# Turning the attention values with VectorE and through DRAM, one item later

## The reference, cut to what matters

```python
x = x + _L1_conv_ref(_gn(x), ...)   # q, k, v of 1024 tokens, masked softmax(q k) v, then Wo
x = x + _L2_conv_ref(_gn(x), ...)   # qkv, softmax(q k + rel_h + rel_w) v per image, then proj
...
s = jnp.einsum('bhqe,bhke->bhqk', q, k) * scale
p = jax.nn.softmax(s, axis=-1)
return jnp.einsum('bhqk,bhke->bhqe', p, v)
```

## Time and profile before

| | |
|---|---|
| median of 3 runs | 1244.69 us |
| the profiled execution's own time | 1246.36 us |
| its span, first to last instruction | 1244.4 us |
| TensorE busy (matmul) | 1216.4 us, 98% |
| weight load, VectorE, ScalarE, GpSimd busy | 78%, 55%, 38%, 52% |
| mean granted TensorE clock | 0.997 of full speed |
| chain that ended last | TensorE 89%, VectorE 5%, ScalarE 2% |
| DMA | 155.03 MB, 125 GB/s mean |

### The profile page before, as it was taken

How to read it: one execution, slowest core, us unless ns; L and a number is a source line. 1 busy time by engine, 2 the same in 40 slices (tenths; PEclk the granted TensorE clock), 3 DMA queues, 4 the chain that set the end, 5 groups by cost and what they waited for, 6 DMA issues and landing times.

```text
span 1244.4 us, 19555 instructions
## 1 busy us (share of the span) xinstructions
PE 1216.4 (98%) x6768; PEld 975.0 (78%) x6768; DVE 690.4 (55%) x1434; ACT 475.1 (38%) x1229; POOL 641.5 (52%) x726
## 2 busy tenths in 40 slices
PE   6999999999999999999999999999999999889998
PEld 4788896478888888888888878777887787668887
DVE  7534444775665433666452578756347776476212
ACT  3611141034645320656341164644206555243212
POOL 4633389256565567555546655555665556464000
PEclk9999999999999999999999999999999999999999
DMA  5211124025564643454645356557535565620012
GB/s 185 84 46 48 34 56 117 8 65 160 154 169 137 184 134 97 127 177 128 185 136 166 86 160 212 180 160 223 168 102 151 175 209 156 205 60 1 29 40 68
DMA packets 129376, 155.03 MB, mean 125 GB/s; under 512 B 30080, under 2 KB 84000, under 8 KB 129280
## 3 DMA queue, kind: packets, MB, share of 16 engines
q1 hardware_dynamic: 118976, 146.92, 39.7%
q10 hardware_dynamic: 10304, 6.88, 1.8%
HBM read 111.81 MB, written 37.75 MB: 120 GB/s over the span
## 4 chain that ended last, share of the span: by engine, by line
PE 89%; DVE 5%; ACT 2%; issue 1%; DMA 1%; SPq 1%; POOL 0%; ACTq 0%; DVEq 0%; POOLq 0%
PE PS L1137 53%; PE PS L682 7%; PE PS L1758 7%; PE PS L1183 4%; PE PS L960 3%; PE PS L969 2%; PE PS L975 2%; PE PS L1227 2%; PE PS L1216 2%; PE PS L1775 2%; PE PS L1247 2%; PE PS L665 1%; PE PS L1197 1%; DVE bst L257 1%; PE PS L700 1%
## 5 line engine op out<-in xcount | busy, mean ns | idle before, releaser
L1137 PE MATMUL PS<-XB,w_hi 128*128 128x512 f32 x1024 | 340.5, 397 | 1.2 <-POOL w_lo L228 1.2
L226 POOL CAST w_hi<-w_raw 128x512 fp32r<-128x512 f32 x195 | 124.2, 637 | 307.5 <-PE PS L1137 213.0
L228 POOL TENSOR_TENSOR w_lo<-w_raw,w_hi 128x512 fp32r<-128x512 f32 x195 | 256.1, 1313 | 15.6
L1137 PEld LDWEIGHTS PS<-XB,w_hi 128*128 128x128 f32 x1024 | 192.2, 188 | 47.1 <-issue 5.0
L1137 PE MATMUL PS<-XB,w_lo 128*128 128x512 f32 x512 | 200.2, 391 | 0.0
L1137 PE MATMUL PS<-XB,part 128*128 128x512 f32 x768 | 190.3, 394 | 0.0
L1137 PEld LDWEIGHTS PS<-XB,part 128*128 128x128 f32 x768 | 141.9, 188 | 32.2 <-issue 2.3
L1373 ACT ACTIVATE part<-PS,nmax 128x256 f32<-128x256 f32 (+1 forms) x256 | 112.2, 443 | 141.6 <-DVE nmax L1485 93.2
L1383 ACT ACTIVATE part<-part,prec 128x256 f32<-128x256 f32 (+1 forms) x256 | 105.8, 476 | 27.7 <-DVE prec L1500 27.7
L228 POOL TENSOR_TENSOR part<-part,part 128x512 fp32r<-128x512 f32 x85 | 111.5, 1312 | 6.8
L1137 PE MATMUL PS<-part,w_hi 128*128 128x512 f32 x344 | 112.9, 395 | 1.5 <-DVE part L1544 1.5
(11 more groups left out here) (136 smaller groups left out, 1884.0 us busy)
## 6 DMA issues: line engine op xcount, KB each, us to landing
w_raw<-in_w SPq DMA_DIRECT2D x187, 256.0 KB, 2.8
part<-in_w SPq DMA_DIRECT2D x85, 256.0 KB, 2.8
turned<-part SPq DMA_DIRECT2D x128, 128.0 KB, 2.9
part<-turned SPq DMA_DIRECT2D x32, 512.0 KB, 5.0
turned<-part SPq DMA_DIRECT2D x128, 96.0 KB, 2.5
part<-turned SPq DMA_DIRECT2D x32, 384.0 KB, 4.0
strips<-part ACTq DMA_DIRECT2D x16, 256.0 KB, 2.7
out_x<-xT SPq DMA_DIRECT2D x16, 256.0 KB, 2.1
```

The lines of the kernel that those rows point to most:

```text
L226: pool.tensor_copy(hi, raw).then_inc(w_hi_done, 1)
L228: pool.tensor_tensor(lo, raw, hi.bitcast(F32), ALU.subtract).then_inc(w_ready, 1)
L1137: m = nc.tensor.matmul(PS[:, bank, :], wt[:, (c % 4) * P:(c % 4) * P + P], rhs(hl, c), start=c == k == 0, stop=c == CK - 1 and k == 2)
```

## The change

The values are no longer turned by TensorE. VectorE turns the projected values straight from PSUM into `vB` in 32x32 blocks (without bias), SP writes them to a DRAM tensor `values` (4 DMAs) and reads them back (1 DMA), and ScalarE copies them into `v` with the blocks in place (`take_v`). The bias of the values is added behind the attention product instead, in `evac_o` and `rest_of_o` (the probabilities of a row sum to one). The products `attend(i - 1)` come behind the values V(i), and in the first item of a stage Q(i + 2) comes ahead of the output blocks. The probabilities of both images lie in one buffer and go out in one set of 4 DMAs of twice the run; `STRIPS_AT` and `PROBS_AT` lie later in SP's order. ScalarE does `evac_relative` ahead of the first two `normalize`. In the tail six banks are used for the last output blocks and five half-blocks come ahead of the last `attend`.

```diff
             take_block(i, "V", range(0 if i else 1, 2))
+            if i + 2 < ITEMS:
+                take_block(i + 2, "Q")
             if s and j == 0:
                 for o in range(CK):
                     take((s - 1, "O", o), STAGES[s - 1][0], "O", o)
-            if i + 2 < ITEMS:
-                take_block(i + 2, "Q")
-            for o in {ITEMS - 2: (0,), ITEMS - 1: (1, 2)}.get(i, ()):
+            for o in {ITEMS - 2: (0,), ITEMS - 1: (1, 2, 3, 4, 5)}.get(i, ()):
                 take((3, "O", o), 2, "O", o, (0,))
...
-    M_AFTER = {(0, 1): (), (1, 1): (0, 1), (2, 1): (2, 3), (3, 0): (4,), (3, 1): (5, 6),
-               (4, 0): (7,), (4, 1): (8, 9), (5, 0): (10, 11), (5, 1): (12,), (6, 0): (13,), (6, 1): (14,), (7, 0): (15,), (7, 1): ()}
+    M_AFTER = {(0, 1): (0, 1), (1, 1): (2, 3), (2, 1): (4,), (3, 1): (5, 6), (4, 1): (7, 8), (5, 1): (9,),
+               (6, 0): (10, 11), (6, 1): (12, 13), (7, 0): (14, 15), (7, 1): ()}
+    M_BANKS = (S + 3, O)
...
-        def turn_values(i):
-            pe.wait_ge(v_evac, i + 1)
-            ...
-            for tt in range(4):
-                m = nc.tensor.transpose(PS[:, turned_bank(i), tt * P:tt * P + P], vT[:, tt * P:tt * P + P], ident[:, :])
-            m.then_inc(v_tr, 1)
...
         for i in range(1, LAST - 1):
             score_block(i)
             project(i + 1, "K", range(CK))
+            project(i, "V", range(CK))
             attend(i - 1, 0)
             attend(i - 1, 1)
-            project(i, "V", range(CK))
+            project(i + 2, "Q", range(CK))
             if i % PAIRS == 0:
                 s = i // PAIRS - 1
-                ...
-                project(i + 2, "Q", range(CK))
-            else:
-                project(i + 2, "Q", range(0, 2))
-                turn_values(i)
-                project(i + 2, "Q", range(2, CK))
+                for o in range(CK):
+                    out_block(s, o, range(CK))
         i = LAST - 1
         score_block(i)
         project(LAST, "K", range(CK))
+        project(i, "V", range(CK))
         attend(i - 1, 0)
         attend(i - 1, 1)
-        project(i, "V", range(CK))
         scores(LAST, 0)
         scores(LAST, 1)
-        out_block(3, 0, range(0, 2))
-        turn_values(i)
-        out_block(3, 0, range(2, 4))
+        out_block(3, 0, range(0, 4))
         project(LAST, "V", range(CK))
+        for o in (1, 2):
+            out_block(3, o, range(0, 4))
         attend(i, 0)
         attend(i, 1)
-        ...
+        for o in (3, 4, 5):
+            out_block(3, o, range(0, 4))
         attend(LAST, 0)
         attend(LAST, 1)
-        for o in range(3):
-            out_block(3, o, range(7, CK))
+        for o in range(6):
+            out_block(3, o, range(4, CK))
             for k in M_AFTER[o, 1]:
                 build_m(k)
-        for o in range(3, CK):
+        for o in range(6, CK):
...
     def attention_act(act):
-        def evac_v(i):
-            ...
+        def take_v(i):
+            act.wait_ge(v_in, 16 * (i + 1))
             if i:
+                act.wait_ge(o_done, 2 * i)
+            dst = v.rearrange("p t (b c) -> p t b c", b=4)
+            nc.scalar.activation(dst, vB.rearrange("p (b t c) -> p t b c", b=4, t=4), ACT.Copy).then_inc(v_ready, 1)
...
             exps(i, 0)
             exps(i, 1)
+            evac_relative(i + 1)
             normalize(i, 0)
             normalize(i, 1)
-            evac_relative(i + 1)
+            if 0 < i < LAST:
+                take_v(i - 1)
             exps(i, 2)
             normalize(i, 2)
+            if i == LAST:
+                take_v(i - 1)
             exps(i, 3)
...
-            if j:
-                evac_o(i - 1)
-            evac_v(i)
             if 1 <= j <= 4:
                 ...
                     norm.head(s + 1, c)
+            if i:
+                evac_o(i - 1)
...
-        def take_v(i):
-            ...
+        def turn_values(i):
+            product_done(dve, (i, "V"))
+            if i:
+                dve.wait_ge(v_ready, i)
+            src = PS[:, bank_of(i, "V"), :].rearrange("p (t q c) -> p t q c", t=4, q=4)
+            dst = vB.rearrange("p (q t c) -> p t q c", q=4, t=4)
+            nc.vector.transpose(dst, src).then_inc(v_turned, 1)
...
             if i < LAST:
                 rest_of_k(i + 1)
-            if j:
+            if i < LAST:
+                turn_values(i)
...
+            if j:
+                rest_of_o(i - 1)
...
-    def probs_to_dram(sp, i, a):
+    def probs_to_dram(sp, i, a=None):
...
+            row = probB[32 * q:32 * q + 32, 0:8 * run].rearrange("p (b r) -> p b r", b=4)
+            at, w = (0, 2 * run) if a is None else (a * run, run)
...
+    def values_to_dram(sp, i):
+        sp.wait_ge(v_turned, i + 1)
+        ...
+        for b in range(4):
+            to = bass.AP(values.tensor, (i % 2) * P * 4 * P + P * b, [[4 * P, 32], [32 * 4 * P, 4], [1, P]])
+            sp.dma_start(to, vB[32 * b:32 * b + 32, :].rearrange("p (q r) -> p q r", q=4)).then_inc(v_out, 16)
+
+    def values_from_dram(sp, i):
+        sp.wait_ge(v_out, 64 * (i + 1))
+        sp.dma_start(vB, values[i % 2, :, :]).then_inc(v_in, 16)
+
+    STRIPS_AT = [slots[(i + 1, "K"), 1] if i < LAST else slots[(i, "V"), 0] for i in range(ITEMS)]
+    PROBS_AT = [slots[(i + 1, "V"), 1] for i in range(LAST - 1)] + [slots[(3, "O", 1), 0], slots[(3, "O", 5), 0]]
...
+                if n == PROBS_AT[i] and i < LAST:
+                    probs_to_dram(sp, i)
+                    values_to_dram(sp, i)
+                if n == PROBS_AT[i] + 1 and i < LAST:
                     probs_from_dram(sp, i, 0)
                     probs_from_dram(sp, i, 1)
+                if n == PROBS_AT[i] + 2 and i < LAST:
+                    values_from_dram(sp, i)
...
-            if n == slots[(3, "O", 5), 0]:
+            if n == slots[(3, "O", 5), 1]:
                 masked_factor(pool, 3)
```

More of the change, by code:

```diff
@@ L774, in later_layers @@
     probT = carve(16384, [P, 2, 4 * N])
-    turned = nc.dram_tensor("turned", (2, 2, P, 4 * N), F32).ap()
+    values = nc.dram_tensor("values", (2, P, 4 * P), F32).ap()
+    turned = nc.dram_tensor("turned", (2, P, 8 * N), F32).ap()
     nmax = sb(outer, "nmax", [P, 4, 2])
@@ L1426, in evac_o @@
             hi, src = o_parts(i)[0], o_source(i)
-            nc.scalar.activation(hi, src, ACT.Copy).then_inc(o_hi, 1)
+            if layer_of(i) == 1:
+                ins = nc.scalar.activation(hi, src, ACT.Copy)
+            else:
+                ins = nc.scalar.activation(hi, src, ACT.Identity, bias=bias[:, 16 + j:17 + j])
+            ins.then_inc(o_hi, 1)
         evac_q(0)
@@ L1433, in attention_act @@
             j, s = i % PAIRS, i // PAIRS
-            if i:
+            if i and (i < PAIRS or j != 1):
                 evac_q(i + 1)
@@ L1455, in attention_act @@
                     norm.head(s + 1, c)
+            if i:
+                evac_o(i - 1)
+            if i and j == 0:
+                evac_q(i + 2)
+        take_v(LAST)
         evac_o(LAST)
@@ L1581, in attention_dve @@
             turn_probs(i, 2)
-            if i and j == 0:
-                rest_of_o(i - 1)
+            if i == LAST:
+                turn_values(i)
             invert_sums(i, 3)
@@ L1587, in attention_dve @@
                 rest_of_k(i + 1)
-            if j:
+            if i < LAST:
+                turn_values(i)
+            if i and j == 0:
                 rest_of_o(i - 1)
-            if i and j == 0:
-                take_v(i)
-            if i and j == 0:
+                rest_of_q(i + 2)
                 for o in range(CK):
@@ L1599, in attention_dve @@
                 norm.group_stats(s + 1)
-            if j or i == 0:
-                take_v(i)
-            if j == 0:
+            if j == 1:
                 norm.coefficients(s + 1)
@@ L1608, in attention_dve @@
                     norm.rest(s + 1, c)
+            if j:
+                rest_of_o(i - 1)
         rest_of_o(LAST)
         for o in range(CK):
-            for k in M_AFTER.get((o, 0), ()):
-                rest_of_m(dve, k)
+            if o >= 6:
+                for k in M_AFTER[o, 0]:
+                    rest_of_m(dve, k)
+                for k in (2 * o - 12, 2 * o - 11):
+                    stats_of(3, k)
             add_out(3, o)
-            if o:
-                stats_of(3, o - 1)
             for k in M_AFTER[o, 1]:
                 rest_of_m(dve, k)
-        stats_of(3, CK - 1)
+        for o in range(4, CK):
+            stats_of(3, o)
         norm.aggregate(5, range(CK), 16)
@@ L1651, in probs_from_dram @@
     def probs_from_dram(sp, i, a):
-        w = 8 * squares(i) * 32
-        sp.wait_ge(p_out[a], 64 * (i + 1))
+        run = 2 * squares(i) * 32
+        if i == LAST and a:
+            sp.wait_ge(p_out[1], 64)
+        else:
+            sp.wait_ge(p_out[0], 64 * (i + 1))
         if i:
             sp.wait_ge(o_done, 2 * i - 1 + a)
```

(3 more changed lines are left out.)

127 lines of the change are left out of this document (55 added, 72 removed).

## The result

The change makes the kernel slower. On one chip the kernel before took 1244.45 us (median of 6 runs, 1242.74 to 1245.58), the changed one 1252.36 us (6 runs, 1249.32 to 1260.02): a ratio of 1.0075, 95% interval 1.0046 to 1.0103. The prediction was 1225.2 us, with 1218 to 1235 as its range. The changed kernel's runs lie further apart than those of before, and its profiled execution, 1260.02 us with a span of 1258.2, is the slowest of them.

What follows compares the result with a forecast made beforehand. TensorE was taken to bound the kernel. 13.2 + 0.3 + 7 (tail) - 1 (norm items) = 19.5 us off the profiled 1246.36 gave 1226.9, named as 1225.2 us for the median; bounds 1219 to 1234, widened to 1218 to 1235.

Steps and rivals of the forecast that it cites:

- What bounds the kernel: Layer-2 attentions: TensorE runs without gap, so anything taken off it there comes off the time.
- Part 1: Four transposes per item leave TensorE: 0.44 us each group, 13.2 us over items 0 to 29.
- Part 2: VectorE and ScalarE: work nearly even, softmax 1.0 to 1.1 us later per layer-2 item, cover just suffices; 1 us charged.
- The 0.1 us charged in each norm item: Eight layer-2 items with norm: VectorE's low part of Q just in time; 0.1 us each (range 0 to 0.9).
- Part 3: SP's queue and DMAs: the values' read lands 6.2 to 8.2 us into the next item and hides, costing nothing.
- 1.5 us was to spare: Layer 2: values landing before ScalarE's `take_v` at 9.7 us of the next item, with 1.5 us or more of cover.
- the values come home late: Rival: read lands 13 us into an item, stops ScalarE 3.3 us, 26 us over eight norm items; 1251 us, chance 0.06.
- 0.68: The chance given to the forecast time and its range.
- The first items of stages swap O and Q blocks ... Nothing: Stages' first items: same work, 5.4 us of Q still cover the evacuation of O; no cost.
- Part 4: Tail, item 30's scores to first channel product, 90.1 us: fewer waits, fewer transposes, clock perhaps held; 7 us less.
- M's waits: Tail: 16 M in ten gaps of 2.72 us, TensorE waiting for VectorE; 2.8 us in all.
- 13.2 and 0.3 us certain: Terms of the sum: 13.2 us from transposes in items 0 to 29, 0.3 from a short wait in item 0.

Runs made afterwards that it cites:

- e4: Changed kernel with only ScalarE's evacuation of the relative products back behind the first two scalings: 1255.7 us, ratio 1.0078 to the kernel before.
- e3: Changed kernel without the values' trip through DRAM (values of other blocks are multiplied): 1233.52 us, ratio 0.9905 to the kernel before.
- e2: Changed kernel with the values' read issued one slot earlier, ahead of the reads of probabilities: 1237.99 us, ratio 0.994 to the kernel before.
- e10: Changed kernel with one edit, Q's block half ahead of and half behind the output blocks: 1253.28 us, ratio 1.0081 to the kernel before.
- e8: Changed kernel with the values' trip made but its read unused and not awaited (values of other blocks are multiplied): 1238.17 us, ratio 0.9957 to the kernel before.
- e6: e3 with Q's block half ahead of and half behind the output blocks: 1224.78 us, ratio 0.9844 to the kernel before.
- e5: e2 for all but the last two items, plus Q's block half ahead of and half behind the output blocks: 1235.01 us, ratio 0.9924.
- e9: e5 with ScalarE's copy of the values moved behind its third scaling: 1234.74 us, ratio 0.9917 to the kernel before.
- e7: Changed kernel with the probabilities written in two sets of four DMAs again, each half the run: 1252.53 us, ratio 1.0051 to the kernel before.

## Why the prediction was wrong

**What bounds the kernel, and Part 1: right.** TensorE was the bound, and 0.44 us per item was to come off. Layer 1's items lost 0.49 us, layer 2's undisturbed items 0.49 to 0.52. The Trainium skill's price for a transpose ("TensorE: Matmul & The Clock Gate", Part 4: PE-mode transpose), is about 275 ns each, which gives an estimate of 1.1 us for four. This case's traces have no such gain: the start-to-start figure of the chain was the one to trust.

**Part 2: durations and times right.** The turn from PSUM takes 706 ns (0.7 taken), the copy 632 ns (0.65). The 0.1 us charged in each norm item didn't come: with the values at home, layer-2 items take 21.78 us. In item 19 of the changed kernel the last turn of probabilities ends 17.1 us into the item and the turn of the values at 18.4, both to the tenth as forecast. e4 rules out the moved evacuation as the source of the loss. What Part 2 didn't see is that behind a stage's first item VectorE starts its sums only 4.5 us into the item (e3), as told below.

**Part 3: the step that failed.** "The value read ... is issued near 24.5 and lands at 28 to 30, which is 6.2 to 8.2 in the next item." For item 19, whose scores start at 748.99, it was issued at 28.9 and landed at 35.4, 13.6 us into the next. The terms one by one, forecast against measured:

- strips read starts at 10.8, was 12.4; eight issues 4.9 us, were 5.68;
- probability writes start at 17.1, were 19.3, though the turn they wait for ended at 17.1: SyncE was busy with the strips to 18.1 and then sent two weight loads; an issue 0.67 us, was 3.80 / 4 = 0.95;
- value writes over at 22.0, were at 26.4 (0.8 us an issue);
- read issued to landed 3.5 to 5.5 us, was 6.45.

Each term was sized by a row of before, with other sizes and fewer transfers under way. No term by itself added more than 3 us, but they all lie on one in-order queue, and the landing inherits all of them: it comes 5.4 to 7.4 us later than forecast, and 1.5 us was to spare. The forecast also took the read's place behind the probabilities as given and never asked what it would share the DMA engines with; e2 shows that this place alone cost 14.4 us. The Trainium skill ("DMA: Bandwidth & Descriptors", Rules for kernel authors) calls transfers under 64 KB mostly overhead. These writes are of just 64 KB, land in 2.4 us, and no run varied their size. Late landing may also feed itself, as a late softmax makes the next probabilities' and values' writes late; that would fit e10, where items 20 and 21 grew as item 18 shrank, but no run tests it.

The rival "the values come home late" had the mechanism: 13 us into an item, ScalarE stopped for 3.3 us (13.6 and 3.82 at item 20). That its 1251 us is near the measured 1252.4 is luck. It had all of the loss in the eight norm items, 3.3 us each. Of the five longest, items 21, 22 and 29 aren't norm items; items 18 and 26 are, but stay long in e8 with no wait for values; and items 19, 20, 27 and 28, norm items too, stay within 0.5 us of the undisturbed. Its chance of 0.06 rested on "DMAs of double size land in 5 us", a median over a quieter queue. A forecast with 1.5 us of margin behind twelve queued issues (four and four writes, two loads, two reads) deserved far less than 0.68.

**"The first items of stages swap O and Q blocks ... Nothing": wrong.** I asked what Q covered for ScalarE (the evacuation of O) and not what it covered for VectorE on the other side (add, statistics, aggregate of the last output block). Restoring half of the cover is worth 8.7 us (e6 against e3), part of it through VectorE's instructions that no longer fall beside GpSimd's. In the changed kernel the loss is in plain sight in items 17, 18, 25 and 26, but repairing it alone gains nothing while the values are late (e10).

**Part 4: right only without the trip.** Forecast 7 us less than 90.1; with the trip left out (e3) the stretch took 81.3 us. With the trip made and its read early it takes 89.5 us in e2 and 86.2 in e5 (where the last two items' reads are late as before): the forecast had no term for a weight half-block that GpSimd splits late, 2.37 us of waiting in e2 and 2.59 in e5. The waits of e3's tail:

```profile
1051.43 1.69 PE L1182 MATMUL PS<-part,part 64*128 64x256 f32 x24 [1.49 <-DVE part L1511]
...
1078.88 1.08 PE L1203 MATMUL PS<-part,part 128*64 128x256 f32 x8 [0.66 <-DMA part<-turned]
1086.89 0.51 PE L1272 MATMUL PS<-ttA,part 96*128 96x256 f32 x2 [0.50 <-DVE part L1749]
```

1.49 us for scores(31) (1.6 forecast) and 0.66 for `attend(31)` (1.0). M's waits are 0.50, 0.39, 0.53 and 0.57, with 0.20 for a weight: 2.2 us where 2.8 was forecast. (The list of waits before left out one of 0.56 us, at 1114.89.) In the changed kernel the first of these waits is 4.29 us, and the stretch falls only to 87.0.

So the sum of 1225.2 us was the price of a kernel without the trip and with the swap covered: e6, 1224.78 us. The trip costs 10.2 us even with its read early and Q split (e5 over e6), and 18.8 us as it was built (the changed kernel over e3). The arithmetic of what left TensorE was sound; what failed was the claim that two things were hidden. The agreement to 0.4 us is partly luck: in e6's profiled execution layer 1 gave 8.2 us where 7.3 was forecast, layer 2 up to item 30 4.4 where 5.2 was, and the tail 9.4 where 7 was.

The range was also too narrow for its own terms. With 13.2 and 0.3 us certain, 0 to 7 us lost in norm items and 2 to 11 gained in the tail, it is 1220 to 1236, not 1219 to 1234. Neither holds the measured time.

The best complete kernels of the study, e5 and e9, compute everything and take 1235.0 and 1234.7 us: 0.8% below the kernel before and 1.4% below the changed one.

## What to carry to other kernels

Where a transfer "hides with 1.5 us to spare", walk its whole in-order queue with issue times from a stretch as busy as the new one will be, and look at what is issued just ahead of it: a small read that an in-order engine waits for belongs ahead of the large ones that nobody needs yet. When two blocks of the bottleneck engine are swapped, ask for every other engine what each block was covering, on both sides. And undo losses in order: a repair may show nothing (e10) while a larger loss still stands.

## What the runs showed of the hardware

**A wait of 3 us on TensorE cost nearly twice its length.** TensorE in the changed kernel, item 18, and two stretches, in the columns of the earlier trace rows, the first with the wait and the second with the same work in item 19:

```profile
726.11 2.77 PE L1234 MATMUL PS<-part,part 64*128 64x64 f32 x24 [3.07 <-issue]
728.81 4.54 PE L1138 MATMUL PS<-XB,part 128*128 128x512 f32 x12
...
750.67 1.53 PE L1234 MATMUL PS<-part,part 64*128 64x64 f32 x24
752.13 3.02 PE L1138 MATMUL PS<-XB,part 128*128 128x512 f32 x12
```

```profile
725.00:730.00 5.00, 3.89 (x27) 3.66 (x28) 4.93 (x10) 1.11 (x5) 0.00 (x0) 0.53 0.81 223
750.00:755.00 5.00, 5.00 (x49) 4.29 (x46) 4.93 (x9) 1.02 (x4) 1.18 (x1) 1.00 0.82 226
```

Behind 3.07 us of idle time the granted clock is 0.53 in the stretch, close to the lower of its levels (1.2 GHz of 2.4), and the relative products take 2.77 us for 1.53, the first 12 of K 4.54 for 3.02. Item 18 is 27.63 us long, 5.84 more than 21.79, for a wait of 3.07. e8 has this wait too, so late values aren't needed for it. Another like it: 3.06 us made item 26 of e3 5.7 us longer. A wait of 1.56 us (item 17, 23.35 us long) cost only itself. But the length of the wait doesn't decide it alone: the same 0.91 us of idle time in item 17 cost 0.91 us in e5, while in e6 the granted clock fell to 0.55 in the 2.5 us from 702.5 on and the item took 24.33 us, 2.55 more than 21.78. Layer 2 as a whole is 27.8 us longer than in e6, with 19.4 us of idle time ahead of its products against 2.2 there. The fallen clock is part of why the losses come in jumps.

**An issue on SyncE's queue isn't a constant.** In layer 2, up to item 30, the writes of probabilities took 0.53 to 0.67 us an issue before and 0.72 to 0.95 in the changed kernel, where each is twice as large. e7 has the small ones again beside the changed kernel's other transfers: 0.52 to 0.62 each. So most of the difference goes with the size, not with the other transfers. The four writes of values right behind them, the same in both, took 1.85 us in item 19 of e7 and 3.20 in that of the changed kernel.

**VectorE can stand still beside GpSimd.** In e3 its L343 took 1.28 us instead of 0.18 when it started 0.06 us after a subtraction of GpSimd, and ended 0.05 us after it. Two such meetings go with TensorE's waits of 3.06 us instead of 1.20. That one engine holds the other is read from these times, not tested.
